# Routed experts by falling row count: 256, 224 or 192 rows by rank, the order computed on the chip

## What is computed

```python
# x: 2048 tokens x 256; 64 experts, FFN = 176, TOP_K = 6, two shared experts
logits = einsum('th,eh->te', x, gate_w)
topk_w, topk_ids = top_k(softmax(logits), 6);  topk_w /= sum(topk_w)
comb = zeros(T, 64).at[arange(T)[:, None], topk_ids].add(topk_w)
g, u = split(einsum('th,efh->tef', x, w_gate_up))     # 176 and 176
act  = silu(g) * u * comb[:, :, None]
routed = einsum('tef,ehf->th', act, w_down)
shared = (silu(x @ ws_g.T) * (x @ ws_u.T)) @ ws_down.T
x = x + tanh(g_ffn[1]) * (routed + shared)
```

## Time and profile before

| what | us |
|---|---|
| runs | 811.56, 807.09, 808.74 |
| median | 808.74 |
| profiled execution, span | 809.0 (808.98 in full) |
| TensorE matmuls busy in it | 660.4 |
| VectorE, ScalarE, GpSimd busy | 483.3, 293.8, 448.0 |

### The profile page before, as it was taken

How to read it: one execution, slowest core, us unless ns; L and a number is a source line. 1 busy time by engine, 2 the same in 40 slices (tenths; PEclk the granted TensorE clock), 3 DMA queues, 4 the chain that set the end, 5 groups by cost and what they waited for, 6 DMA issues and landing times.

```text
span 809.0 us, 12013 instructions
## 1 busy us (share of the span) xinstructions
PE 660.4 (82%) x3068; PEld 501.3 (62%) x3068; DVE 483.3 (60%) x1590; ACT 293.8 (36%) x641; POOL 448.0 (55%) x481
## 2 busy tenths in 40 slices
PE   3688984764998767988887659999999999999930
PEld 2354542433887646766666548888888888888720
DVE  3887776997687777777773615445434543454322
ACT  2146666864344423444433212323332333233200
POOL 2577877120344313766666614676776677667752
PEclk9699998887999978999999789999999999999975
DMA  6347545586888664545425266999999999999587
GB/s 226 123 134 249 199 156 208 171 279 237 290 316 304 229 209 140 193 162 183 173 94 200 92 218 174 241 242 237 260 250 230 234 258 254 231 240 233 88 178 227
DMA packets 94691, 169.07 MB, mean 209 GB/s; under 512 B 10944, under 2 KB 60032, under 8 KB 94656
## 3 DMA queue, kind: packets, MB, share of 16 engines
q1 hardware_dynamic: 70368, 137.05, 50.6%
q0 software_dynamic: 23424, 30.70, 20.6%
q10 hardware_dynamic: 864, 0.93, 0.3%
HBM read 94.30 MB, written 74.33 MB: 208 GB/s over the span
## 4 chain that ended last, share of the span: by engine, by line
PE 55%; DVE 17%; issue 9%; POOL 7%; DMA 5%; ACT 2%; another core or an unknown queue 2%; DVEq 1%; SPq 1%; POOLq 0%; ACTq 0%
PE psum L1027 13%; PE psum L1040 7%; PE psum L1031 7%; PE psum L798 5%; PE psum L874 5%; POOL xs_rows L694 5%; PE psum L1045 4%; PE psum L1015 4%; DVE hh L1573 2%; PE psum L953 2%; PE psum L770 2%; PE psum L865 2%; PE psum L780 1%; DMA acc<-hh,toki 1%
## 5 line engine op out<-in xcount | busy, mean ns | idle before, releaser
L731 POOL DMA_INDIRECT acc<-hh,toki x128 | 198.8, 1553 | 101.5 <-DVE hh L1868 62.3
L1868 DVE TENSOR_SCALAR hh<-psum,wtok 128x256 f32<-128x256 f32 x128 | 56.0, 480 | 155.8 <-DMA acc<-hh,toki 98.7
L694 POOL DMA_INDIRECT xs_rows<-Z,slot x96 | 96.6, 1006 | 58.4 <-DVE slot L1749 32.4
L1027 PE MATMUL psum<-qT,Z 128*128 128x256 f32 x512 | 122.7, 383 | 3.5 <-DVE hh L1858 3.5
L1027 PEld LDWEIGHTS psum<-qT,Z 128*128 128x128 f32 x512 | 93.1, 192 | 14.5 <-issue 4.4
L618 POOL TENSOR_TENSOR rstd<-mv,neghalf 128x1 f32<-128x1 f32 (+1 forms) x48 | 36.7, 765 | 75.1 <-DVE mv L1364 75.1
L1298 ACT ACTIVATE qT<-psum 128x512 f32<-128x512 f32 x64 | 38.2, 598 | 102.2 <-PE psum L1015 100.3
L798 PE MATMUL psum<-wt,hTs 128*128 128x512 f32 x128 | 61.8, 627 | 9.4 <-ACT hTs L1122 9.4
L1031 PE MATMUL psum<-qT,Z 128*112 128x256 f32 x256 | 66.6, 383 | 0.0
L1040 PE MATMUL psum<-Z,hh 128*128 128x256 f32 x256 | 61.0, 381 | 1.2 <-DVE hh L1858 1.2
L953 PE MATMUL psum<-qT,wt 128*128 128x256 f32 (+1 forms) x192 | 51.4, 424 | 8.9 <-DVE H L1754 8.9
(11 more groups left out here) (316 smaller groups left out, 1253.6 us busy)
## 6 DMA issues: line engine op xcount, KB each, us to landing
Z<-in_wexp SPq DMA_DIRECT2D x66, 496.0 KB
xs_rows<-fill SPq DMA_DIRECT2D x64, 272.0 KB, 3.3
Z<-xs_rows SPq DMA_DIRECT2D x64, 272.0 KB
kv_rows<-Z SPq DMA_DIRECT2D x12, 688.0 KB, 3.8
kvb<-kv_rows SPq DMA_DIRECT2D x8, 688.0 KB
Z<-co_rows SPq DMA_DIRECT2D x8, 688.0 KB
Z<-kv_rows SPq DMA_DIRECT2D x8, 688.0 KB
acc<-fill SPq DMA_DIRECT2D x4, 1024.0 KB, 8.9
```

The lines of the kernel that those rows point to most:

```text
L694: pool.indirect_dma_start(out=xs_rows[:, :], out_offset=bass.IndirectOffsetOnAxis(ap=slot[:, t, k:k + 1], axis=0), in_=H[:, t, :], in_offs ...
L731: pool.indirect_dma_start(out=acc[s % 2][:, :], out_offset=bass.IndirectOffsetOnAxis(ap=toki[:, g, j:j + 1], axis=0), in_=y_sb[:, s, j, :] ...
L1027: m = pe.matmul(pA[par][:, g * CAP:(g + 1) * CAP], wgu_sb[:, s, k, g * P:(g + 1) * P], xT[:, par, k, :], start=(k == 0), stop=(k == 1))
L1868: m = dve.tensor_scalar(y_sb[:, s, j, :], pY[par][:, j * D:(j + 1) * D], wtok[:, g, j:j + 1], None, ALU.mult)
```

## The change

The counts that TensorE sums after the last routing step are now used a second time. VectorE builds for each expert the key 64 x count - number, counts how many keys are greater (`rank_e`) and marks its rank in a one-hot row (`by_rank`); TensorE multiplies it with the expert numbers (`pid_row`) and gives `order_i` (one row, read by SP) and `order_f` (on all partitions, read by `weights` in place of `iota_e`). SP loads rows and weights of the expert at rank `r`, for which it reads one number of `order_i` into a register before each load.

Ranks 0 to 15 process 256 rows (`p` = 128 a half), ranks 16 to 31 224 (`p` = 112), ranks 32 to 63 192 (`p` = 96). Loads, transposes, up products, SiLU, hidden products, scaling and adds all use `p`; the down product streams 256 features as before. `p` is fixed in the code, so the loops over groups of eight experts are cut into several (`PHASES`). The overflow plan takes each expert's own row limit (`cap_e`, `cap_row`). GpSimd copies `gcol` itself, VectorE's loop over the padding is gone, and SP waits for the padding before the overflow blocks' loads.

```diff
-    LAG = 4
+    PARTS = (128, 128, 112, 112, 96, 96, 96, 96)
+    STEPS = ((16, 32.0), (32, 32.0))
+    PHASES = ((1, 2), (2, 3), (3, 4), (4, 5), (5, 8))
...
-            def load_rows(e, s):
-                sp.dma_start(xs_sb[:, s].rearrange("p b d -> p (b d)"),
-                             rows_v[e, 0:CAP, :].rearrange("(p b) d -> p (b d)", b=2)).then_inc(xs_in[s], 16)
+            def expert_at(r):
+                alone(sp, "sp")
+                return sp.value_load(order_i[0:1, bass.ds(r, 1)], min_val=0, max_val=E - 1)
+
+            def load_rows(r, s, p):
+                sp.dma_start(xs_sb[0:p, s].rearrange("p b d -> p (b d)"),
+                             rows_v[expert_at(r), 0:2 * p, :].rearrange("(p b) d -> p (b d)", b=2)).then_inc(xs_in[s], 16)
 
 
             sp.wait_ge(o3_ready, NH)
+            sp.wait_ge(ov_ready, 1)
             for s in range(4):
-                load_weights(s, s, w_in[s])
+                load_weights(expert_at(s), s, w_in[s])
             sp.wait_ge(scattered, 16 * NT * K)
             for s in range(4):
-                load_rows(s, s)
+                load_rows(s, s, PARTS[0])
             for s in range(4, WS):
-                load_weights(s, s, w_in[s])
...
+            def refill(i, near, far):
                 for g in range(0, WS, 2):
                     for j in range(2):
-                        next_rows(WS * i + 4 + g + j, (g + j) % 4)
+                        next_rows(WS * i + 4 + g + j, (g + j) % 4, near if g < 4 else far)
                     for j in range(2):
 
                         sp.wait_ge(y_done, WS * i + g + j + 1)
-                        load_weights(WS * i + WS + g + j, g + j, w_in[g + j])
...
-            sp.wait_ge(ov_ready, 1)
+                        load_weights(expert_at(WS * i + WS + g + j), g + j, w_in[g + j])
+
+            for lo_, hi_ in ((0, 1), (1, 2), (2, 3), (3, 4), (4, 7)):
+                with sp.Fori(lo_, hi_) as i:
+                    refill(i, PARTS[lo_], PARTS[lo_ + 1])
...
+            sp.wait_ge(ov_ready, 2)
...
+            sp.wait_ge(padded, 32 * n)
+            alone(sp, "sp")
...
+            pool.wait_ge(hidT_full, NT)
+            pool.iota(pid_row[:, :], pattern=[[0, P]], base=0, channel_multiplier=1,
+                      allow_small_or_imprecise_dtypes=True).then_inc(c_done, 1)
...
-            pool.wait_ge(ov_ready, 1)
+            pool.wait_ge(ov_ready, 2)
+                pool.tensor_copy(gcol[:, :], gidx[:, bass.ds(2 * b, 2)]).then_inc(gcol_ready, 1)
...
-                        out=acc[s % 2][:, :], out_offset=bass.IndirectOffsetOnAxis(ap=toki[:, g, j:j + 1], axis=0),
-                        in_=y_sb[:, s, j, :], in_offset=None, compute_op=ALU.add).then_inc(added[s % 2], 16)
+                        out=acc[s % 2][:, :], out_offset=bass.IndirectOffsetOnAxis(ap=toki[0:p, g, j:j + 1], axis=0),
+                        in_=y_sb[0:p, s, j, :], in_offset=None, compute_op=ALU.add).then_inc(added[s % 2], 16)
-                add_rows(0, g, True)
-            with pool.Fori(1, E // 8) as i:
-                for g in range(8):
-                    add_rows(i, g, False)
+                add_rows(0, g, PARTS[0], True)
+            for lo_, hi_ in PHASES:
+                with pool.Fori(lo_, hi_) as i:
...
+            pe.wait_ge(ov_vals, 1)
+            pe.matmul(pT[1][:, 2 * E:3 * E], pid_row[:, :], by_rank[:, :], start=True, stop=True).then_inc(ov_sums, 1)
             shared_up(NPAIR - 1, 2)
-            pe.wait_ge(ov_vals, 1)
+            pe.wait_ge(ov_vals, 2)
+            pe.matmul(pT[1][:, 3 * E:4 * E], cap_row[:, :], ident[0:E, 0:E], start=True, stop=True)
             pe.matmul(pT[1][:, 0:E], nb_b[:, :], trii[:, :], start=True, stop=True)
             pe.matmul(pT[1][:, E:2 * E], nb_b[:, :], tri[0:E, 0:E], start=True, stop=True).then_inc(ov_sums, 1)
-            pe.wait_ge(ov_vals, 2)
+            pe.wait_ge(ov_vals, 3)
...
-            pe.wait_ge(ov_ready, 1)
+            pe.wait_ge(ov_ready, 2)
...
-                        m = pe.transpose(pT[par][:, k * CAP + j * P:k * CAP + (j + 1) * P],
-                                         xs_sb[:, s, j, k * P:(k + 1) * P], ident[:, :])
+                        m = pe.transpose(pT[par][:, (2 * k + j) * p:(2 * k + j + 1) * p],
+                                         xs_sb[0:p, s, j, k * P:(k + 1) * P], ident[0:p, 0:p])
...
-                        m = pe.matmul(pA[par][:, g * CAP:(g + 1) * CAP], wgu_sb[:, s, k, g * P:(g + 1) * P],
-                                      xT[:, par, k, :], start=(k == 0), stop=(k == 1))
+                        m = pe.matmul(pA[par][:, g * CAP:g * CAP + 2 * p], wgu_sb[:, s, k, g * P:(g + 1) * P],
+                                      xT[:, par, k, 0:2 * p], start=(k == 0), stop=(k == 1))
...
-                    m = pe.matmul(pC[par][0:GU - 2 * P, 0:CAP], wgu_sb[:, s, k, 2 * P:GU],
-                                  xT[:, par, k, :], start=(k == 0), stop=(k == 1))
+                    m = pe.matmul(pC[par][0:GU - 2 * P, 0:2 * p], wgu_sb[:, s, k, 2 * P:GU],
+                                  xT[:, par, k, 0:2 * p], start=(k == 0), stop=(k == 1))
...
-                        pe.matmul(pY[q][:, j * D:(j + 1) * D], hid0[:, q, j * P:(j + 1) * P],
+                        pe.matmul(pY[q][0:p, j * D:(j + 1) * D], hid0[:, q, j * p:(j + 1) * p],
...
-                        m = pe.matmul(pY[q][:, j * D:(j + 1) * D], hid1[r, q, j * P:(j + 1) * P],
+                        m = pe.matmul(pY[q][0:p, j * D:(j + 1) * D], hid1[r, q, j * p:(j + 1) * p],
...
-            with pe.Fori(1, E // WS) as i:
-                for g in range(0, WS, 2):
-                    pair(i, g, False)
-            up(E // WS - 1, WS - 1, False)
-            down_pair(E // WS - 1, WS - 2)
+                pair(0, g, p0, p0)
+            for lo_, hi_ in PHASES:
+                with pe.Fori(lo_, hi_) as i:
+                    for g in range(0, WS, 2):
+                        pair(i, g, PARTS[lo_], PARTS[lo_ - 1])
...
+            dve.wait_ge(ov_sums, 1)
+            dve.scalar_tensor_tensor(key_e[:, :], pT[0][0:E, 0:1], float(E), pid[0:E, :], ALU.mult, ALU.subtract)
+            link(dve.scalar_tensor_tensor(keys[:, 0, :], pT[0][0:E, P:P + E], float(E), iota_e[0:E, :], ALU.mult, ALU.subtract))
+            link(dve.tensor_scalar(keys[:, 1, :], keys[:, 0, :], key_e[:, 0:1], 0.0, ALU.is_gt, ALU.add, accum_out=rank_e[:, 0:1]))
+            dve.tensor_scalar(by_rank[:, :], iota_e[0:E, :], rank_e[:, 0:1], None, ALU.is_equal).then_inc(ov_vals, 1)
+            dve.tensor_copy(ov_c[:, 0, :], pT[0][:, P:P + E])
+            link(dve.tensor_copy(cnt_f[:, :], pT[0][0:E, 0:P]))
+            dve.wait_ge(ov_sums, 2)
+            dve.tensor_copy(order_i[:, :], pT[1][0:1, 2 * E:3 * E]).then_inc(ov_ready, 1)
+            dve.tensor_copy(order_f[:, :], pT[1][:, 2 * E:3 * E])
             shared_hidden(NPAIR - 1, 0)
             shared_hidden(NPAIR - 1, 1)
-            dve.wait_ge(ov_sums, 1)
-            link(dve.tensor_copy(cnt_f[:, :], pT[0][0:E, 0:P]))
-            dve.tensor_copy(ov_c[:, 0, :], pT[0][:, P:P + E])
+            link(dve.tensor_scalar(cap_e[:, 0:1], rank_e[:, 0:1], float(STEPS[0][0]), STEPS[0][1], ALU.is_ge, ALU.mult))
+            link(dve.tensor_scalar(cap_e[:, 1:2], rank_e[:, 0:1], float(STEPS[1][0]), STEPS[1][1], ALU.is_ge, ALU.mult))
+            link(dve.tensor_tensor(cap_e[:, 0:1], cap_e[:, 0:1], cap_e[:, 1:2], ALU.add))
+            link(dve.tensor_scalar(cap_e[:, 1:2], cap_e[:, 0:1], -1.0, float(CAP), ALU.mult, ALU.add))
+            dve.tensor_scalar(cap_row[:, :], onesf[0:E, :], cap_e[:, 1:2], None, ALU.mult)
+            link(dve.tensor_scalar(cnt_f[:, :], cnt_f[:, :], cap_e[:, 0:1], None, ALU.add))
...
-            dve.wait_ge(ov_sums, 2)
+            dve.wait_ge(ov_sums, 3)
+            dve.tensor_copy(ov_c[:, 2, :], pT[1][:, 3 * E:4 * E])
...
+            link(dve.scalar_tensor_tensor(ov_w[:, 3, :], iota_e[:, :], ov_s[:, 1:2], ov_c[:, 2, :], ALU.is_equal, ALU.mult, accum_out=ov_s[:, 9:10]))
...
-            link(dve.tensor_scalar(ov_s[:, 6:7], ov_s[:, 4:5], ov_s[:, 5:6], float(CAP), ALU.add, ALU.add))
+            link(dve.tensor_scalar(ov_s[:, 6:7], ov_s[:, 4:5], ov_s[:, 5:6], ov_s[:, 9:10], ALU.add, ALU.add))
...
-            with dve.Fori(0, n) as b:
-                dve.tensor_copy(gcol[:, :], gidx[:, bass.ds(2 * b, 2)]).then_inc(gcol_ready, 1)
-                dve.wait_ge(padded, 32 * b + 32)
-                alone(dve, "dve")
...
-                    dve.scalar_tensor_tensor(wsel[:, s, j, :], xs_sb[:, s, j, CE:CE + K], iota_e[:, bass.ds(e, 1)],
-                                             xs_sb[:, s, j, CW:CW + K], ALU.is_equal, ALU.mult, accum_out=wtok[:, g, j:j + 1])
...
+                    dve.scalar_tensor_tensor(wsel[0:p, s, j, :], xs_sb[0:p, s, j, CE:CE + K], order_f[0:p, bass.ds(e, 1)],
+                                             xs_sb[0:p, s, j, CW:CW + K], ALU.is_equal, ALU.mult, accum_out=wtok[0:p, g, j:j + 1])
...
```

(4 more changed lines are left out.)

152 lines of the change are left out of this document (82 added, 70 removed).

## The result

| | before | after |
|---|---|---|
| median of 19 runs | 810.67 us | 805.96 us |
| lowest to highest | 807.09 to 814.60 | 802.59 to 816.40 |
| profiled execution, span | 809.0 | 811.3 |

The ratio is 0.9948 with a 95% interval of 0.9929 to 0.9967: faster by half a percent, where 3.8% was forecast. (The run of 816.40 us fell in a slower state of the chip and is left out of the ratio.) The profiled execution of the changed kernel (813.14 us in full) is 7 us above its median, so its trace is read for mechanisms, and sizes are taken from ratios of runs.

A forecast was written before the change was run, and what follows sets the result against it. TensorE, never idle in the routed experts' pairs, was taken as the bound. 808.98 us less 25.8 (narrower matmuls) and 4.7 (start) gave 778.5, for the median 778.2, stated as 778; range 771 to 790, to hold 8 in 10.

The forecast's parts named there:

- Term 1: Routed experts, ranks 16 to 63: narrower up-product matmuls shorten TensorE's pairs from 9.00 to 8.35 and 7.71 us, saving 25.8 us.
- if TensorE remains the bound: Condition on the 25.8 us saving in the expert loop: GpSimd, its adds and the DMA engines keep up with shorter pairs.
- the load sets it: Transposes in expert pairs: the 128-column weight load sets their pace, so narrowing gains 0; upper bound 4.6 us in all.
- what is hidden: Ranking's 4 to 5 us before the experts and SP's 2.4 us of register loads a pair cost nothing, being covered by waiting.
- GpSimd follows: Expert loop: GpSimd's four accumulating DMAs take 7.44 us a pair at most, 5.9 if they shrink, under TensorE's 7.71.
- DMA follows: Expert loop: DMA engines need 7.6 us a pair against 7.71, and 8.3 against 8.35; cost taken 0, at most 5.8 us.
- rival (a): Expert loop: weight packets make the DMA engines the bound, pairs 8.0 and 8.5 us, total 784 to 790; chance 0.07.
- Rival (b): Expert loop: adds' landing sets the pace, rising from 5.6 to 6.5 us, pairs 8.66 us, total 796; chance 0.06.
- (c): Expert loop: adds landing as slowly as 7.39 us make pairs 9.55 us, slower than before, total 817; chance 0.05.
- (d): Overflow loop: experts exceeding 224 or 192 rows add blocks, each two a further turn of some 21 us; chance 0.02.
- (e): Expert loop: transposes, second products (L1045) and GpSimd all shrink with the rows, total below 771 us; chance 0.02.
- Term 2: Start of the experts: padding wait and TensorE's 3.50 us stall go, clock stays up, one register load costs 0.6; net 4.7 us.

The follow-up runs named there:

- four accumulators: Changed kernel with row loads issued before weights and four DRAM accumulators instead of two (only two summed): 0.9673, 782.4 us; with rows late 0.9933.
- rows first: Changed kernel with SP issuing the row loads before the wait for second products and the weight loads in the refill loop: 0.9849, 795.6 us.
- full width: Changed kernel with every rank at 256 rows, ranking and register loads kept: 1.0168, 822.8 us with rows late; 0.9998 with rows issued ahead of weights.

## Why the prediction was wrong

**Term 1, size of the matmuls: right.** Pairs at 192 rows are 7.54 us where TensorE doesn't wait (predicted 7.71), at 224 rows 8.27 (8.35). The rest of the difference is mostly the transposes, for which nothing was taken: at 96 rows four take 0.39 and 0.33 us instead of 0.49 and 0.44, 0.21 a pair, close to the 0.23 that the prediction gave as its bound "if they did scale with columns". Load (PEld) and matmul records of the transposes, at 128 rows before and at 96 rows with four accumulators (shortest, median and longest in ns):

```profile
L1015 PEld LDWEIGHTS psum<-ident,Z x224: 139/141/143, 500.3 to 746.6; 128*128 128x128 f32 x112
L1015 PE MATMUL psum<-ident,Z x224: 272/273/329, 500.3 to 746.7; 128*128 128x128 f32 x112
...
L1046 PEld LDWEIGHTS psum<-ident,Z x92: 137/140/143, 641.4 to 724.6; 96*128 96x128 f32 x92
L1046 PE MATMUL psum<-ident,Z x92: 243/246/301, 641.5 to 724.6; 96*128 96x96 f32 x92
```

The load's record stays the same, the matmul's falls by 27 ns for 32 streamed columns, 0.84 ns a column, the slope that the prediction had taken for the up products. So the reading "the load sets it" was wrong, and L930's 0.118 was no guide: its loads last 192 ns in the trace before, the transposes' 141. (Rows and streamed columns fall together in every run, so that the two are told apart only by these records.) The Trainium skill's rule (TensorE: Matmul & The Clock Gate, LDWEIGHTS) of a load time independent of rows agrees with the load records, though not with their 141 ns, where it has 107; that the transposes gain nothing did not follow from it. The term was worth 8 x 0.73 + 16 x 1.46 = 29 us, and the run with four accumulators has it: its loop is 247.94 us, 29.4 less than before.

**Term 1, "if TensorE remains the bound": wrong.** The step that failed is in the paragraph on what is hidden: "In the loop SP does four register loads a pair, 4 x 0.6 = 2.4 us in an engine that otherwise waits for TensorE; the rows it fetches are needed two pairs later". The rows are issued after the wait for one pair's products and needed with only one pair between. The idle time of SP was real, but it lay before `y_done`, and the register loads came behind it. With that in the sum the 10.1 us loop would have been there before the run, and the alternation with it: a pair may not start earlier than 10.1 us after the end of the pair two before. The evidence offered, "TensorE never waited", hid a margin of about 1 us. In the two profiled executions the sum is: 2.0 us won at the start, 1.25 lost in the loop, 2.3 in the tail and 0.7 ahead of the router's sum, together the 2.3 us by which the changed kernel's span is longer.

**GpSimd follows: right** (1.43 us an add at 96 rows, 6.9 a pair). **DMA follows: right**, and rival (a) was none.

**Rival (b), 796 us, had the right mechanism** and came out as the second limit: with rows first the landing that was followed took 6.3 us (median of 28: 6.2) where it assumed 6.5. That rows first gave 795.6 is partly luck: its loop is 12.6 us shorter than before, where (b) has 8.2, and its start gives 1.4 us, where (b) has 4.7. "That wait ended within TensorE's period each time" was true at 9.00 and not at 7.54. It didn't decide the changed kernel itself (four accumulators gave it nothing), so its 6% were not what happened either. (c) needs landings of 7.04 us and more in pair after pair; with rows first single landings reached 7.2 (561.07) and 8.3, most did not. (d): no second turn of the overflow loop. (e): transposes and adds did shrink with the rows (0.2 us a pair, 1.55 to 1.43 us an add), the second products didn't, and neither set the time.

**Term 2: mechanism right, size partly.** The padding wait and the stall behind it are gone, and alone they give 3.9 us to the first second products and 0.5% of the time. The changed kernel keeps 2.0 of 36.1. Predicted was one register load of 0.59 us; the row issue came 1.9 us later, and the first two row loads stand 1.16 us apart (471.15 and 472.31) instead of 0.4. The order itself was there at 454.64, 2.1 us after the sum, in time; but the first weights, for which nothing was taken, now meet the scatters. The overflow plan behind the order ended at 469.32, 7.8 us later than before, where 4 to 5 were predicted; nobody waited for it, since GpSimd's first add, at 491.45, waited for VectorE's scaling.

**What would show it**: the prediction named idle time behind row loads as the mark of rival (a). The mark was right, its cause wasn't: bytes were not in the way, the order of issues was.

Open: the profiled execution of the changed kernel has a tail (last pair to end) 2.3 us longer than before; it is 1 to 6 us longer in every other narrow kernel, and not longer by more than 0.2 in those at full width; it wasn't taken apart. What sends TensorE's clock down behind some waits and not behind others. And why SP's instructions take 0.70 us beside the last scatters.

## What to carry to other kernels

Before shortening a loop's bound, write down for every prefetch when it is issued, behind which wait, and when its data is needed; the margin of a load that never made anyone wait can be one microsecond. In a queue that serves near and far needs, issue what is needed next first: here that order was worth 1.0% with two accumulators, 1.7% at full width and 2.6% with four. When two limits lie behind each other, removing either alone shows nothing or half; try both together before dropping either.

## What was not expected of the hardware

- A DMA share of 0.99 at 246 GB/s became 1.01 at 254 GB/s when TensorE asked for more.
- A float32 transpose's pace fell with the rows, 0.11 us at 128 and 0.083 at 96, although the record of its load stayed at 0.14 us.
- SP took 0.70 us for each piece of an issue or register load between 460 and 470 us, and mostly 0.02 to 0.36 elsewhere.
- A wait of 2.1 us on rows was followed by matmuls at the 1.2 GHz level (eight in 2.6 us instead of 1.33), and four pairs became 11.4 to 11.8 us where the waits explain 9.7 to 10.0; a wait of 2.0 us in the same execution was not followed by it.
